# Column degrees from diagonals of products of the masked counts, in the middle stage of a graph kernel

## The chip, the cores and the metric

The kernel runs on one core of a Trainium2 chip. The metric is the device time of one execution in microseconds (us), the median of several runs. Engines are named as the profile names them: PE is TensorE (PEld its weight loads), DVE is VectorE, ACT is ScalarE, POOL is GpSimd, SP is SyncE, whose queue (SPq) issues the DMAs.

## What is computed

```python
# x (64, 128, 1024), adj (128, 128), bias (128), gumbel (1024*1024, 2)
h = relu(layernorm(x, axis=-1))                  # 64 batches of T=128 by N=1024
avg = h.mean(over the 64 batches)                # one vector of 128 per node, N=1024 nodes
x_norm = avg / norm(avg)
sim = (x_norm @ x_norm.T + 1) / 2
A = (sim + gumbel[:, 0] > 1 - sim + gumbel[:, 1])        # 1024 x 1024, zeros and ones
sym = clip(A + A.T, 0, 1); nmask = clip(sym + eye, 0, 1)
common = nmask @ nmask.T                         # counts of common neighbours
struct = where(sym and common > 1, common**2 / common.max(), 0)
W = A * struct
deg = W.sum(axis=0)                              # sum over the rows of each column
Wn = deg**-0.5 [row] * W * deg**-0.5 [column]
out = x + transpose(Wn applied to (h.T @ adj)) + bias
```

W is the square of (A times common), up to a constant. So a column's degree is the sum over rows of (A times common) squared: this is the quantity whose computation changes here.

## The kernel before

The work has three stages.

**Pass 1** (the span's start to about 108 us) reads all of x once, normalises, applies ReLU and sums the 64 batches into `S`; batches 0, 8, ... are also multiplied by the weight in fp32 (`kept`, 8 MATMULs of 128x128 per batch) and kept in `xw_res`.

**The middle stage** (about 108 to 193 us) makes the 1024x1024 matrix. It lies in 8 blocks of 128 rows.
- Comparisons: for each block `c`, PE makes `ps_sim` (fp32, 128x512), DVE first subtracts the two gumbel halves of a later block (`margin_of`) and then compares (`adjm`, L1007). PE's block `c` waits for DVE's comparison `c-2`, since `ps_sim` has two buffers.
- Symmetrised mask: PE adds a block and its transposed parts (`sym_start`, `sym_part`), ACT makes the even blocks of `nmask` (L441), DVE the odd ones (L1011), each with a row sum.
- `lonely_loops_dropped`: 8 small DVE operations on the diagonal blocks of `adjm` (L1035).
- Counts: PE multiplies `nmask` by itself, 16 MATMULs of 128x512 per block (L813), in the order `CHUNKS` = 0, 4, 1, 5, 2, 6, 3, 7. DVE multiplies each block with `adjm` into `masked` (`mask`, L1052).
- Degrees before the change: since DVE and ACT can only sum along a row, the columns' sums are had from turned blocks. As `common` is symmetric, column block `c` of (A times common), transposed, is `common` block `c` times A's transposed block. PE turns `adjm` (`turn_adj`, 8 MATMULs of 128x128, L778), ACT copies that to SBUF (`turned`, L545), DVE multiplies it with the counts a second time (`mask_t`, L1061), ACT squares and sums along the row (`degree_of`, L551).
- Then DVE bounds the degrees (L1066, L1067), POOL takes the power -1/4 (`roots`, L389: 6 columns, then 2), DVE finishes `qf` (L1072), PE spreads `qf` as rows over all partitions (`q_row`, L834), DVE multiplies (`rooted`, L1116), ACT squares and rounds (L594, L598), DVE takes the rest (`low`, L1122). PE gets zero products (`stay_awake`, L667) while it waits: `stay_awake(..., 5)` ahead of `q_row`, `(..., 8)` ahead of the first product. One fp32 MATMUL of the program is two records of the profile.
- Woven into this: the first pairs of batches of pass 2 are prepared. For a batch `j`, ACT makes ReLU twice (`relu2`, fp32 and fp16, L459, L469), DVE takes the fp16 rest (`h_low`, L1031), PE does 24 fp16 MATMULs (`xw_of`, L795), ACT copies the result to `z` (`z_of`, L489) and makes its fp16 part (`y_high_first`, L494; `y_high`, L508), DVE its rest (`y_low_first`, L1047; `y_low`, L1042).
- The maximum of the counts: `turn(0)`, `top_of(0)` on DVE, `spread(0)`, then `k0` on DVE (L1079, semaphore `top_count_read`).

**Pass 2** (from 193 us) multiplies 32 pairs of batches by the matrix, seven products per pair; almost all of it is PE's L852.

Each engine runs its own list in program order; the order is written by hand in each engine's function, with semaphores between them. SP's queue holds, behind the gumbel loads (L272), the loads of x for batches 1 to 7 (`x_first`, L286), which wait for all eight comparisons.

Of the kernel before, what the change touches and what calls it, by code (L numbers as in the profile page):

```python
# [28 lines left out]
BF16 = mybir.dt.bfloat16  # L29
# [23 lines left out]
def gnn_kernel(nc, x, adj, bias, gumbel, out):  # L53
# [14 lines left out]
    with ExitStack() as ctx:  # L68
# [16 lines left out]
        ident16 = sb("ident16", [P, P], BF16)  # L85
# [38 lines left out]
        adjm = xring[:, 0:4, :].bitcast(BF16).rearrange("p a (b n) -> p (a b) n", b=2)  # L124
        nmask = xring[:, 4:8, :].bitcast(BF16).rearrange("p a (b n) -> p (a b) n", b=2)
# [10 lines left out]
        def tile16(half, mat, k, dt=F16):  # L136
            return a16[:, half, mat, 2 * k:2 * k + 2, :].bitcast(dt).rearrange("p c n -> p (c n)")

        masked = [tile16(half, mat, k) for half, mat in ((0, 5), (1, 5), (1, 3), (1, 4)) for k in (0, 1)]
        adjt = [tile16(e // 4, 1 + e // 2 % 2, e % 2, BF16) for e in range(C)]  # L140
        masked_t = [tile16(0, 0, k) for k in (0, 1)]
        square_t = [a16[:, 0, m, :, :].bitcast(F32).rearrange("p c n -> p (c n)") for m in (3, 4)]
# [23 lines left out]
        ps_adjt = pair[2]  # L166
# [44 lines left out]
        s_adjtp = sem("adj_transposed")  # L211
        s_adjt = sem("adj_transposed_in_sbuf")
        s_m = sem("masked_count_ready")
        s_mt = sem("masked_count_transposed_ready")
# [37 lines left out]
        CHUNKS = [c + HC * k for c in range(HC) for k in (0, 1)]  # L252
# [7 lines left out]
        def _(sp):  # L260
# [49 lines left out]
        def _(pool):  # L310
# [85 lines left out]
            roots(0, 0, 6)  # L396
            roots(1, 6, C)
# [4 lines left out]
        def _(act):  # L402
# [20 lines left out]
            act.sem_inc(s_v, 3)  # L423
            def relus(i, except_for=()):
# [14 lines left out]
            for c in range(0, C, 2):  # L439
                act.wait_ge(s_sym, c + 1)  # L440
                nc.scalar.activation(nmask[:, c, :], ps_sym[c % 4], ACT.Sign,  # L441
                                     accum_out=row_count[:, c:c + 1]).then_inc(s_mask[0], 1)

# [99 lines left out]
            def turned(e):  # L543
                act.wait_ge(s_adjtp, e + 1)
                nc.scalar.activation(adjt[e], ps_adjt, ACT.Copy).then_inc(s_adjt, 1)  # L545

            def degree_of(e):
                act.wait_ge(s_mt, e + 1)
                if e >= 2:
                    act.wait_ge(s_deg, e - 1)  # L550
                nc.scalar.activation(square_t[e % 2], masked_t[e % 2], ACT.Square,  # L551
                                     accum_out=degree[:, e:e + 1]).then_inc(s_deg, 1)

            relu2(0, 0, 1)
            z_of(0, 0, 0)
            turned(0)
            y_high_first(0)
            turned(1)
            degree_of(0)
            relu2(0, 1, 0)  # L560
            z_of(0, 0, 1)
            y_high_first(1)
            turned(2)
            degree_of(1)
            relu2(0, 1, 1)
            turned(3)
            degree_of(2)
            y_high_first(2)
            y_high_first(3)
            turned(4)  # L570
            degree_of(3)
            z_of(0, 1, 0)
            y_high(0, 1, 0)
            turned(5)
            degree_of(4)
            z_of(0, 1, 1)
            y_high(0, 1, 1)
            turned(6)
            degree_of(5)
            y_high(0, 1, 2)  # L580
            turned(7)
            degree_of(6)
            relu2_wide(0, 2, 0)
            degree_of(7)
            relu2_high(0, 2, 0)
# [63 lines left out]
        def _(pe):  # L649
# [65 lines left out]
            for half in (0, 1):  # L715
                pe.wait_ge(s_rn, half + 1)
                bcast(ps_bc, rnorm, half).then_inc(s_bc, 1)
            for c in range(C):
# [7 lines left out]
                mm.then_inc(s_sim, 1)  # L726

# [14 lines left out]
            for k in range(C):  # L742
                pe.wait_ge(s_adj, k + 1)
                if k < 2:
# [26 lines left out]
            def turn_adj(e):  # L771

                if e == 0:
                    pe.wait_ge(s_edge, C)
                pe.wait_ge(s_adjt, e)
                c = CHUNKS[e]
                for k in range(C):
                    mm = nc.tensor.matmul(ps_adjt[:, k * P:(k + 1) * P], adjm[:, k, c * P:(c + 1) * P], ident16[:],  # L778
                                          start=True, stop=True, skip_group_check=True)
                mm.then_inc(s_adjtp, 1)  # L780

            def xw_of(i, q, b):
# [6 lines left out]
                if j > 1 or not isinstance(i, int) or i > 0:  # L789
                    pe.wait_ge(s_z, BODY * i + j)  # L790
                else:
# [10 lines left out]
            for e, c in enumerate(CHUNKS):  # L802
                if e >= 2:
                    pe.wait_ge(s_m, e - 1)
                    pe.wait_ge(s_mt, e - 1)
                for k in range(C):
                    if e == 0:
                        for n in {c % 2, k % 2}:
                            pe.wait_ge(s_mask[n], max(c, k) // 2 + 1)
                    if e >= 1 and k == HC:  # L810
                        turn_adj(e)
                    for m in range(2):
# [465 lines left out]
```

## Time and profile before

| | us |
|---|---|
| median of 3 runs | 853.83 (852.73 to 854.52) |
| profiled execution, its own time | 853.35 |
| its span, first to last instruction | 851.6 |
| busy in the span: PE, DVE, ACT, POOL | 821.1, 583.3, 508.4, 309.3 |
| mean granted TensorE clock | 0.994 of full speed |
| middle stage, comparisons' first MATMUL to first product of pass 2 | 115.08 to 193.12 |

The times in the rows count from the span's start. A timeline row gives start and duration, line, operation, operands and count; in brackets stands how long the engine had been idle and who released it. A duration holds the engine's pipeline tail, so that two instructions in a row overlap a little, and the step from start to start is what an instruction costs in a row of them. What lies outside the span (853.35 - 851.6 = 1.75 us) is taken as unchanged.

### The profile page before, as it was taken

The numbers are of one execution on the slowest core, as the hardware profiler recorded it, in microseconds if no ns is written. First come the engines' busy times: TensorE is split into PE (matmuls) and PEld (weight loads), VectorE is DVE, ScalarE is ACT, GpSimd is POOL, SyncE is SP. The second block draws the span as 40 slices with busy tenths as digits, with TensorE's granted clock in tenths as the row PEclk, the third lists the DMA queues.
The fourth block names the chain that finished last, engine by engine and source line by source line (L and its number), as shares of the span: only waits on it lengthen the run. The fifth ranks groups of instructions, "written<-read, shape, count | busy, mean of one in ns | idle before, by whom it ended". The sixth has DMA issues, their size and how long they took to land.

```text
span 851.6 us, 13546 instructions
## 1 busy us (share of the span) xinstructions
PE 821.1 (96%) x4739; PEld 429.6 (50%) x4746; DVE 583.3 (68%) x679; ACT 508.4 (60%) x530; POOL 309.3 (36%) x255
## 2 busy tenths in 40 slices
PE   4999999969999999999999999999999999999997
PEld 3545455554454555555455555554555455545553
DVE  7999986789986665666566666656665666566652
ACT  3888714879645665665566566656664555565531
POOL 4888710030433333333333333334333433333320
PEclk9999999989999999999999999999999999999999
DMA  8999913100553333333322223222222222233111
GB/s 346 408 409 345 421 46 124 50 1 1 214 183 126 106 109 107 124 106 108 103 99 99 99 99 99 99 99 99 99 99 99 99 99 99 99 101 111 60 50 74
DMA packets 30121, 113.14 MB, mean 133 GB/s; under 512 B 3472, under 2 KB 3600, under 8 KB 29072
## 3 DMA queue, kind: packets, MB, share of 16 engines
q1 hardware_dynamic: 30096, 112.80, 36.6%
q8 instruction: 16, 0.26, 0.1%
q14 instruction: 9, 0.07, 0.0%
HBM read 79.23 MB, written 33.55 MB: 132 GB/s over the span
## 4 chain that ended last, share of the span: by engine, by line
PE 80%; DVE 13%; issue 3%; ACT 2%; DMA 1%; DVEq 0%; SPq 0%; ACTq 0%
PE ps L852 65%; PE ps L795 8%; DVE stats L944 8%; PE ps L867 2%; PE ps L813 1%; PE ps L667 1%; DVE moments L950 1%; PE ps L724 1%; DMA out_dram<-obuf 1%; DVE ybuf L965 1%; DVE xring L1007 1%; DVE obuf L1198 1%; DVE ybuf L1042 0%; PE ps L738 0%; PE ps L731 0%
## 5 line engine op out<-in xcount | busy, mean ns | idle before, releaser
L852 PE MATMUL ps<-a,ybuf 128*128 128x512 f16 x2604 | 570.9, 379 | 0.5 <-ACT obuf L522 0.5
L852 PEld LDWEIGHTS ps<-a,ybuf 128*128 128x128 f16 x2604 | 252.6, 98 | 295.6 <-ACT obuf L522 1.0
L1042 DVE TENSOR_TENSOR ybuf<-zbuf,ybuf 128x1024 f16<-128x1024 f32 x124 | 164.5, 1327 | 157.4 <-ACT ybuf L508 157.4
L380 POOL TENSOR_TENSOR zbuf<-zbuf 128x512 f32<-128x512 f32 x31 | 40.9, 1318 | 444.1 <-ACT zbuf L489 444.1
L508 ACT ACTIVATE ybuf<-zbuf 128x1024 f16<-128x1024 f32 x124 | 117.8, 950 | 115.4 <-POOL zbuf L385 99.9
L522 ACT ACTIVATE obuf<-ps,bias_sb,w_out 128x512 f32<-128x512 f32 x62 | 47.9, 772 | 116.9 <-PE ps L852 111.7
L1031 DVE TENSOR_TENSOR hring<-hring 128x1024 f16<-128x1024 f32 x56 | 68.5, 1224 | 55.8 <-ACT hring L469 55.8
L795 PEld LDWEIGHTS ps<-w,hring 128*128 128x128 f16 x1344 | 79.5, 98 | 14.9 <-issue 2.4
L795 PE MATMUL ps<-w,hring 128*128 128x128 f16 x1344 | 84.2, 219 | 1.9 <-ACT zbuf L489 1.5
L1198 DVE TENSOR_TENSOR obuf<-obuf,xring 128x1024 f32<-128x1024 f32 x64 | 80.4, 1258 | 2.7
L383 POOL TENSOR_TENSOR zbuf<-zbuf 128x512 f32<-128x512 f32 x31 | 68.8, 2220 | 0.0
L489 ACT ACTIVATE zbuf<-ps 128x1024 f32<-128x1024 f32 x56 | 57.3, 1023 | 19.4 <-PE ps L795 19.2
L385 POOL TENSOR_TENSOR zbuf<-zbuf 128x512 f32<-128x512 f32 x31 | 67.8, 2186 | 0.0
L459 ACT ACTIVATE hring<-xring,nbias,rstd 128x1024 f32<-128x1024 f32 x49 | 60.1, 1227 | 0.0
L469 ACT ACTIVATE hring<-xring,nbias,rstd 128x1024 f16<-128x1024 f32 x49 | 60.1, 1227 | 0.0
L382 POOL TENSOR_TENSOR zbuf<-zbuf 128x512 f32<-128x512 f32 x31 | 50.8, 1638 | 2.4
L944 DVE BATCH_NORM_STATS2 stats<-xring 128x6 f32<-128x512 f32 x64 | 38.9, 671 | 0.7 <-issue 0.7
L696 PE MATMUL ps<-hring,ident 128*128 128x512 f32 x76 | 35.0, 607 | 0.3 <-ACT hring L412 0.3
L944 DVE BATCH_NORM_STATS2 stats<-ybuf 128x6 f32<-128x512 f32 x56 | 34.0, 666 | 0.0
L522 ACT ACTIVATE p<-ps,bias_sb,w_out 128x512 f32<-128x512 f32 x31 | 24.0, 773 | 10.4 <-PE ps L852 10.4
L1203 DVE SCALAR_TENSOR_TENSOR obuf<-ps,w_out,obuf 128x512 f32<-128x512 f32 x31 | 23.2, 750 | 9.8 <-PE ps L852 9.7
L696 PE MATMUL ps<-zbuf,ident 128*128 128x512 f32 x60 | 28.2, 602 | 1.7 <-ACT zbuf L412 1.5
(133 smaller groups left out, 673.1 us busy)
## 6 DMA issues: line engine op xcount, KB each, us to landing
xring<-in_x_dram SPq DMA_DIRECT2D x96, 512.0 KB, 4.6
out_dram<-obuf SPq DMA_DIRECT2D x64, 512.0 KB, 2.9
ybuf<-in_x_dram SPq DMA_DIRECT2D x28, 512.0 KB, 8.3
a<-in_L_gnn_gumbel_dram SPq DMA_DIRECT2D x7, 1024.0 KB, 15.9
obuf<-in_x_dram SPq DMA_DIRECT2D x11, 512.0 KB, 5.7
obuf<-in_L_gnn_gumbel_dram SPq DMA_DIRECT2D x1, 1024.0 KB, 23.9
w<-in_adj_dram SPq DMA_DIRECT2D x1, 64.0 KB, 1.9
bias_sb<-in_L_gnn_bias_dram SPq DMA_DIRECT2D x1, 0.5 KB, 2.1
```

The source lines that it names most:

```text
L383: nc.gpsimd.tensor_tensor(z[:, 6, :], z[:, 1, :], z[:, 0, :], ALU.subtract).then_inc(s_zs, 1)
L385: nc.gpsimd.tensor_tensor(z[:, 7, :], z[:, 2, :], z[:, 5, :], ALU.subtract).then_inc(s_zs, 1)
L459: nc.scalar.activation(h32, src, ACT.Relu, bias=nbias[:, bass.ds(t, 1)], scale=rstd[:, bass.ds(t, 1)]).then_inc(s_h32, 1)
L508: nc.scalar.activation(y16[:, q % 2, 0, a:a + n, :], z[:, a + 1:a + 1 + n, :], ACT.Copy).then_inc(s_yhi, 1)
L522: nc.scalar.activation(dst, src, ACT.Identity, bias=bias_sb[:, 0:1], scale=w_out[:, 0:1]).then_inc(s_v, 1)
L696: mm = nc.tensor.matmul(ps_avg[:, m], ident[:], h[:, m], start=False, stop=True, skip_group_check=True)
L795: mm = nc.tensor.matmul(ps_xw2[:, c * P:(c + 1) * P], h16[b][:, hk, c * P:(c + 1) * P], w16[:, wk, :], start=(hk == wk == 0), stop=(hk == ...
L852: mm = nc.tensor.matmul(bank[q % 2], y16[:, q % 2, yk, u, c * P:(c + 1) * P], a16[:, ak, mat, c, :], start=(start and c == yk == ak == 0), ...
L944: nc.vector.bn_stats(stats[:, j % 4, 6 * m:6 * m + 6], x1[j][:, m * H:(m + 1) * H]).then_inc(s_bn, 1)
L1031: nc.vector.tensor_tensor(h16[b][:, 1, :], h32, h16[b][:, 0, :], ALU.subtract).then_inc(s_hlo, 1)
L1042: nc.vector.tensor_tensor(y16[:, q % 2, 1, a:a + n, :], z[:, a + 1:a + 1 + n, :], y16[:, q % 2, 0, a:a + n, :], ALU.subtract).then_inc(s_y, 1)
L1198: nc.vector.tensor_tensor(ob, ob, xring[:, j, :], ALU.add).then_inc(s_out, 1)
```

## The change

1. **No turned adjacency.** `turn_adj`, `turned`, `mask_t` and ACT's `degree_of` go. Counts are made in the order 0 to 7 in full blocks. For each masked block, PE multiplies each of its 8 column blocks of 128x128 with itself (`squared`, 64 MATMULs in all) and sums over the blocks in PSUM: the diagonals of the 8 sums in `ps_diag` are the columns' degrees. DVE reads each diagonal with an identity and a sum along the row (new `degree_of`, 8 operations of 128x128).
2. The last masked block is made in two halves; the degrees' bounds and roots are split 4 and 4; `stay_awake` ahead of `q_row` goes from 5 to 10.
3. **Batch 1 in fp32.** Its load (`x_first[1]`) is issued when pass 1's sums are done and not after the comparisons. ACT makes its ReLU once (`first_h`), PE does 8 fp32 MATMULs with `w_unit` (`first_xw`), two behind each of the comparison blocks 2 to 5, and ACT and DVE make the first pair's `z` and `y` before and between the mask blocks. Batch 1's `relu2`, `h_low` and its 24 fp16 MATMULs go.
4. `adjm`, `nmask` and `ident16` are fp16 and no longer bf16 (both 16 bits).

```diff
@@ sync
+            sp.wait_ge(s_hpe, NT * (TRIPS1 + 1) - 2)
+            sp.dma_start(x_first[1], x[1]).then_inc(s_xf[1], 16)
             sp.wait_ge(s_adj, C)
-            for j in range(1, BODY):
+            for j in range(2, BODY):
@@ gpsimd
-            roots(0, 0, 6)
-            roots(1, 6, C)
+            roots(0, 0, HC)
+            roots(1, HC, C)
@@ scalar
-            relu2(0, 0, 1)
             z_of(0, 0, 0)
-            turned(0)
+            act.wait_ge(s_xf[1], 16)
+            nc.scalar.activation(first_h, x_first[1], ACT.Relu, bias=nbias[:, 1:2],
+                                 scale=rstd[:, 1:2]).then_inc(s_hhi, 1)
             y_high_first(0)
...
+            for c in range(0, C, 2):
+                act.wait_ge(s_sym, c + 1)
+                nc.scalar.activation(nmask[:, c, :], ps_sym[c % 4], ACT.Sign,
+                                     accum_out=row_count[:, c:c + 1]).then_inc(s_mask[0], 1)
@@ tensor
+            def first_xw(n):
+
+                pe.wait_ge(s_hhi, 1)
+                for c in (2 * n, 2 * n + 1):
+                    mm = nc.tensor.matmul(ps_xw2[:, c * P:(c + 1) * P], first_h[:, c * P:(c + 1) * P], w_unit[:],
+                                          start=True, stop=True, skip_group_check=True)
+                return mm
...
+                if 2 <= c < 6:
+                    mm = first_xw(c - 2)
+                    if c == 5:
+                        mm.then_inc(s_xw2, 1)
...
+            def squared(c, half):
+
+                pe.wait_ge(s_m, c + 1 + (half if c == C - 1 else 0))
+                for k in range(half * HC, (half + 1) * HC):
+                    mk = masked[c][:, k * P:(k + 1) * P]
+                    mm = nc.tensor.matmul(ps_diag[:, k * P:(k + 1) * P], mk, mk, start=(c == 0 and k % HC == 0),
+                                          stop=(c == C - 1), skip_group_check=True)
+                return mm
+
+            counted(0).then_inc(s_com, 1)
+            turn(0)
+            for c in range(1, C):
+                counted(c).then_inc(s_com, 1)
+                if c >= 2:
+                    for half in (0, 1):
+                        squared(c - 2, half)
+                if c == 1:
                     spread(0)
-                    xw_of(0, 0, 1)
-                if e == 3:
                     xw_of(0, 1, 0)
-                if e == 4:
+                if c == 3:
                     xw_of(0, 1, 1)
-            pe.wait_ge(s_m, C)
-            stay_awake(ps[:, 3, 0:P], 5)
+            for half in (0, 1):
+                squared(C - 2, half)
+            for half in (0, 1):
+                squared(C - 1, half).then_inc(s_diag, 1)
+            stay_awake(ps[:, 3, 0:P], 10)
@@ vector
             for c in range(1, C, 2):
+                y_low_first(c // 2)
                 dve.wait_ge(s_sym, c + 1)
...
+            def degree_of(c):
+
+                dve.wait_ge(s_diag, c // HC + 1)
+                m = slice(c * P, (c + 1) * P)
+                nc.vector.scalar_tensor_tensor(out=squares[:, m], in0=ps_diag[:, m], scalar=1.0, in1=ident[:],
+                                               op0=ALU.mult, op1=ALU.mult,
+                                               accum_out=degree[:, c:c + 1]).then_inc(s_deg, 1)
...
+            h_low(0, 1, 0)
             dve.wait_ge(s_edge, C)
             top_of(0)
             mask(0)
-            h_low(0, 0, 1)
...
-            mask_t(7)
-            mask(7)
-            root(0, 0, 6)
+            mask(7, LO)
+            mask(7, HI)
+            for c in range(HC):
+                degree_of(c)
+            bound(0, 0, HC)
+            for c in range(HC, C):
+                degree_of(c)
+            root(0, 0, HC)
+            bound(1, HC, C)
+            root(1, HC, C)
```

How the instructions stand on PE in the last three comparison blocks, before and then with the change (L724 before is L705 now, L731 and L733 are L716 and L718, L695 is `first_xw`):

```order
L724 MATMUL ps<-hring 128x512 [waits adj_ready]
L724 MATMUL ps<-hring 128x512
L724 MATMUL ps<-hring 128x512 [waits adj_ready]
L724 MATMUL ps<-hring 128x512
L724 MATMUL ps<-hring 128x512 [waits adj_ready]
L724 MATMUL ps<-hring 128x512
L731 MATMUL ps<-xring,ident 128x512 [waits adj_ready]
L731 MATMUL ps<-xring,ident 128x512
L733 MATMUL ps<-ident 128x128
L731 MATMUL ps<-xring,ident 128x512 [waits adj_ready]
```

```order
L705 MATMUL ps<-hring 128x512 [waits adj_ready]
L705 MATMUL ps<-hring 128x512
L695 MATMUL ps<-w_unit,hring 128x128 [waits h_high_ready]
L695 MATMUL ps<-w_unit,hring 128x128
L705 MATMUL ps<-hring 128x512 [waits adj_ready]
L705 MATMUL ps<-hring 128x512
L705 MATMUL ps<-hring 128x512 [waits adj_ready]
L705 MATMUL ps<-hring 128x512
L716 MATMUL ps<-xring,ident 128x512 [waits adj_ready]
L716 MATMUL ps<-xring,ident 128x512
L718 MATMUL ps<-ident 128x128
L716 MATMUL ps<-xring,ident 128x512 [waits z_ready,adj_ready]
```

Two fp32 MATMULs stand behind a block of comparisons, four times, and the second `sym_start` also waits for ACT's second `z_of`.

PE from the first block's maximum to the next counts, before and then with the change (L813, the counts, are L786 now; L796 is `squared`, L770 is `xw_of`):

```order
L764 MATMUL ps<-ident,col 1x128 [waits column_maxima_ready]
L778 MATMUL ps<-ident,xring 128x128 [waits adj_transposed_in_sbuf,lonely_loops_dropped]
L778 MATMUL ps<-ident,xring 128x128 x7
L813 MATMUL ps<-xring 128x512 x8
L778 MATMUL ps<-ident,xring 128x128 [waits adj_transposed_in_sbuf]
L778 MATMUL ps<-ident,xring 128x128 x7
L813 MATMUL ps<-xring 128x512 x8
L768 MATMUL ps<-top,ones 128x1 [waits top_ready]
L795 MATMUL ps<-w,hring 128x128 [waits top_count_read,h_low_ready]
```

```order
L751 MATMUL ps<-ident,col 1x128 [waits column_maxima_ready]
L786 MATMUL ps<-xring 128x512 x16
L755 MATMUL ps<-top,ones 128x1 [waits top_ready]
L770 MATMUL ps<-w,hring 128x128 [waits top_count_read,z_ready,h_low_ready]
L770 MATMUL ps<-w,hring 128x128 x23
L786 MATMUL ps<-xring 128x512 [waits masked_count_ready]
L786 MATMUL ps<-xring 128x512 x15
L796 MATMUL ps<-a 128x128 [waits masked_count_ready]
L796 MATMUL ps<-a 128x128 x3
```

A block's squares stand behind the counts of the block two later. DVE from the last masked block to `qf`, before and then with the change (`degree_of` is L1046, `mask` L1039):

```order
L1066 TENSOR_SCALAR degree_min<-degree 128x6 [waits degree_ready]
L1067 TENSOR_SCALAR has_deg<-degree 128x6
L1061 SCALAR_TENSOR_TENSOR a<-ps,a 128x1024 [waits degree_ready,adj_transposed_in_sbuf,common_ready]
L1052 SCALAR_TENSOR_TENSOR a<-ps,xring 128x1024 [waits common_ready]
L1072 TENSOR_TENSOR qf<-q_raw,has_deg 128x6 [waits q_raw_ready,degree_bounded]
```

```order
L1039 SCALAR_TENSOR_TENSOR a<-ps,xring 128x512 [waits common_ready] x2
L1046 SCALAR_TENSOR_TENSOR a,degree<-ps,ident 128x128 [waits column_squares_ready] x4
L1052 TENSOR_SCALAR degree_min<-degree 128x4 [waits degree_ready]
L1053 TENSOR_SCALAR has_deg<-degree 128x4
L1046 SCALAR_TENSOR_TENSOR a,degree<-ps,ident 128x128 [waits column_squares_ready] x4
L1058 TENSOR_TENSOR qf<-q_raw,has_deg 128x4 [waits q_raw_ready,degree_bounded]
```

Two full multiplications behind the last counts have become two halves of one and eight small ones.

## Rows read from the trace of the kernel before

**Rows 1.** Page, busy time of each engine in the span, its share and instructions
```profile
PE 821.1 (96%) x4739; PEld 429.6 (50%) x4746; DVE 583.3 (68%) x679; ACT 508.4 (60%) x530; POOL 309.3 (36%) x255
```

**Rows 2.** Chain of waits, end of the middle stage: start us, us, what
```profile
179.46 2.50 PE ps L667 x10
...
185.34 2.57 ACT xring L594 x4
...
221.77 1.34 PE ps L795 x24
```

**Rows 3.** Timeline of PE, pass 1's last fp32 products and the comparisons
```profile
106.07 1.95 PE L682 MATMUL ps<-w_unit,hring 128*128 128x128 f32 x16
...
122.97 1.98 PE L724 MATMUL ps<-hring 128*128 128x512 f32 x4 [0.28 <-DVE xring L1007]
...
127.50 3.70 PE L724 MATMUL ps<-hring 128*128 128x512 f32 x8 [0.28 <-DVE xring L1007]
```

**Rows 4.** Timeline of DVE, comparisons, masks and the dropped loops
```profile
133.11 1.23 DVE L1011 TENSOR_SCALAR_CACHE_REDUCE xring<-ps 128x1024 bf16<-128x1024 f32 x1 [0.64 <-PE ps L738]
134.26 0.08 DVE L1011 DVE_READ_ACCUMULATOR xring<-ps 128x1 f32 x1
134.98 1.23 DVE L1011 TENSOR_SCALAR_CACHE_REDUCE xring<-ps 128x1024 bf16<-128x1024 f32 x1 [0.63 <-PE ps L738]
...
140.26 2.19 DVE L1035 SCALAR_TENSOR_TENSOR xring<-ident,alone,xring 128x128 bf16<-128x128 bf16 x8
```

**Rows 5.** Timeline of PE, the counts
```profile
138.51 3.62 PE L813 MATMUL ps<-xring 128*128 128x512 bf16 x16
...
147.67 1.50 PE L795 MATMUL ps<-w,hring 128*128 128x128 f16 x24 [0.34 <-DVE k L1079]
...
163.75 1.50 PE L795 MATMUL ps<-w,hring 128*128 128x128 f16 x24 [1.53 <-ACT zbuf L489]
...
166.81 0.61 PE L778 MATMUL ps<-ident,xring 128*128 128x128 bf16 x8
167.26 3.62 PE L813 MATMUL ps<-xring 128*128 128x512 bf16 x16
170.71 0.61 PE L778 MATMUL ps<-ident,xring 128*128 128x128 bf16 x8
...
175.06 1.89 PE L813 MATMUL ps<-xring 128*128 128x512 bf16 x8
```

**Rows 6.** Timeline of DVE, from the last counts to the first rooted rows
```profile
149.85 0.68 DVE L1047 TENSOR_TENSOR ybuf<-zbuf,ybuf 128x512 f16<-128x512 f32 x1
...
180.64 0.16 DVE L1072 TENSOR_TENSOR qf<-q_raw,has_deg 128x2 f32<-128x2 f32 x1 [0.89 <-POOL q_raw L389]
...
180.91 1.23 DVE L1031 TENSOR_TENSOR hring<-hring 128x1024 f16<-128x1024 f32 x1
183.20 0.75 DVE L1116 SCALAR_TENSOR_TENSOR xring<-a,qf,ps 128x512 f32<-128x512 f16 x1 [1.06 <-PE ps L834]
```

**Rows 7.** Timeline of POOL, the roots
```profile
177.23 1.34 POOL L389 TENSOR_TENSOR q_raw<-degree_min,neg_quarter 128x6 f32<-128x6 f32 x1 [0.78 <-DVE has_deg L1067]
179.84 0.70 POOL L389 TENSOR_TENSOR q_raw<-degree_min,neg_quarter 128x2 f32<-128x2 f32 x1 [1.27 <-DVE has_deg L1067]
```

**Rows 8.** Stretches of 0.5 us: us, PE busy (instructions), PEclk, DMA share, GB/s
```profile
179.00:179.50 0.50, 0.04 (x1) 0.57 0.00 0
...
182.50:183.00 0.50, 0.50 (x7) 1.00 0.00 0
```

**Rows 9.** A stretch's busy us (instructions): PE, PEld, DVE, ACT, POOL; PEclk, DMA
```profile
214.00:240.00 26.00, 25.99 (x156) 13.05 (x154) 25.96 (x19) 14.17 (x15) 8.73 (x4) 1.00 0.67 246
```

**Rows 10.** Loads of x for batches 1 to 7 (L286), issue to landing
```profile
DMA to landing us min/median/max: 3.3/4.1/6.6
```

**Rows 11.** Loads of the gumbel values (L272), first and last start, issue to landing
```profile
L272 SPq DMA_DIRECT2D obuf<-in_L_gnn_gumbel_dram x1: 432/432/432, 87.6 to 87.6; - x1
...
DMA to landing us min/median/max: 9.9/16.9/23.9
```

More of the change, by code:

```diff
@@ L135, in gnn_kernel, with tile16 @@
         acc = zbuf[:, 0, :]
-        def tile16(half, mat, k, dt=F16):
-            return a16[:, half, mat, 2 * k:2 * k + 2, :].bitcast(dt).rearrange("p c n -> p (c n)")
+        def tile16(half, mat, k):
+            return a16[:, half, mat, 2 * k:2 * k + 2, :].rearrange("p c n -> p (c n)")
         masked = [tile16(half, mat, k) for half, mat in ((0, 5), (1, 5), (1, 3), (1, 4)) for k in (0, 1)]
-        adjt = [tile16(e // 4, 1 + e // 2 % 2, e % 2, BF16) for e in range(C)]
-        masked_t = [tile16(0, 0, k) for k in (0, 1)]
-        square_t = [a16[:, 0, m, :, :].bitcast(F32).rearrange("p c n -> p (c n)") for m in (3, 4)]
+        squares = a16[:, 0, 0, :, :].bitcast(F32).rearrange("p c n -> p (c n)")
+        first_h = hring[:, 0, :]
         rows_hi, rows_lo = xring[:, 4:8, :], xring[:, 0:4, :]
@@ L438, in _ @@
             keep(NK * TRIPS1 - 1)
[L439 to L442, printed above, removed]
             def relu2_wide(i, q, b):
@@ L743, in _ @@
                 pe.wait_ge(s_adj, k + 1)
+                if k == 1:
+                    pe.wait_ge(s_z, 2)
                 if k < 2:
@@ L788, in xw_of @@
                 pe.wait_ge(s_hlo, (BODY - 1) * i + j + 1)
-                if j > 1 or not isinstance(i, int) or i > 0:
-                    pe.wait_ge(s_z, BODY * i + j)
-                else:
+                pe.wait_ge(s_z, BODY * i + j)
+                if isinstance(i, int) and i == 0 and j == 2:
                     pe.wait_ge(s_cnt, 1)
@@ L801, in _, with counted @@
             pe.wait_ge(s_mask[1], 3)
[L802 to L805, printed above, removed]
+            def counted(c):
+                if c >= 2:
+                    pe.wait_ge(s_m, c - 1)
                 for k in range(C):
[L807 to L812, printed above, removed]
-                        mm = nc.tensor.matmul(ps_com[e % 2][:, m * H:(m + 1) * H], nmask[:, k, c * P:(c + 1) * P],
+                    if c == 0:
+                        for n in {0, k % 2}:
+                            pe.wait_ge(s_mask[n], k // 2 + 1)
+                    for m in (0, 1):
+                        mm = nc.tensor.matmul(ps_com[c % 2][:, m * H:(m + 1) * H], nmask[:, k, c * P:(c + 1) * P],
@@ L1007, in _, with y_low_first @@
                 nc.vector.tensor_tensor(adjm[:, c, :], ps_sim[c % 2], margin[c], ALU.is_gt).then_inc(s_adj, 1)
+            def y_low_first(u):
+                dve.wait_ge(s_yhi, u + 1)
+                nc.vector.tensor_tensor(y16[:, 0, 1, u, :], z[:, (u + 1) % 4, :], y16[:, 0, 0, u, :],
+                                        ALU.subtract).then_inc(s_y, 1)
             for c in range(1, C, 2):
+                y_low_first(c // 2)
                 dve.wait_ge(s_sym, c + 1)
@@ L1083, in _ @@
                                     ALU.mult).then_inc(s_cnt, 1)
+            h_low(0, 1, 1)
             mask(1)
-            y_low_first(0)
-            mask_t(1)
-            h_low(0, 1, 0)
+            y_low(0, 1, 0)
             mask(2)
-            mask_t(2)
-            y_low_first(1)
             mask(3)
-            mask_t(3)
-            h_low(0, 1, 1)
-            y_low_first(2)
-            y_low_first(3)
             mask(4)
-            mask_t(4)
+            y_low(0, 1, 1)
             mask(5)
-            mask_t(5)
-            y_low(0, 1, 0)
             mask(6)
-            mask_t(6)
-            y_low(0, 1, 1)
-            bound(0, 0, 6)
-            mask_t(7)
-            mask(7)
-            root(0, 0, 6)
-            bound(1, 6, C)
-            root(1, 6, C)
+            mask(7, LO)
[8 more added lines that the diff above has]
+            root(1, HC, C)
             dve.wait_ge(s_q, 2)
@@ L1113, in rooted @@
             def rooted(rows, k, half, c):
-                e, m = 2 * c + k, (LO, HI)[half]
+                e, m = HC * k + c, (LO, HI)[half]
                 nc.vector.scalar_tensor_tensor(out=rows[:, c, m], in0=masked[e][:, m], scalar=qf[:, e:e + 1],
```

91 lines of the change are left out of this document (19 added, 72 removed).

## Prediction

> **What bounds the kernel now.** The busy row comes first [rows 1]: PE is busy 96% of the span, so time is won only where PE works on less or waits less. The chain of waits then tells where the middle stage hangs: at its end the chain alternates between DVE, PE's zero products and ACT [rows 2], and behind it stands pass 2, PE's own. The stretch 214 to 240 has DVE busy for 25.96 and PE for 25.99 of 26 us [rows 9]: whatever arrives earlier at the first rooted rows is carried through pass 2's start by two full engines, and neither has slack that would eat it. So I price the change by one event, DVE's first `rooted` at 183.20 [rows 6], and by the first ACT square behind `kappa`, at 185.34 [rows 2]; both now end on what PE and DVE do after the last counts. The unit is the profiled execution, 853.35 us, 0.48 below the median; I take the same shift for both.
>
> **Comparisons.** Each block of four records lasts 1.98, a double block 3.70 [rows 3]: four records cost 1.72 and 0.26 is tail. With the idle 0.28 behind it a gap of 0.54 us is free per block while DVE sets the pace. Sixteen fp32 records of 128x128 last 1.95 [rows 3], so the four of one `first_xw` cost 0.43. They fit with 0.11 to spare: cost 0. If they did not fit at all, they would cost 4 x 0.43 = 1.7; below 0 they cannot go, as DVE's pace stays. I take 0, by the gap, which is of the same place. What is queued behind them are the comparisons themselves.
>
> Their input is batch 1's load, issued at about 106.1, when PE's last sum is done, behind the last gumbel load, which starts at 87.6 and lands 23.9 later, at 111.5 [rows 11]. A load of this size takes 3.3 to 6.6 from issue to landing [rows 10]. It lands at 111.5 to 118, and PE asks for it at 120.3 (a block of 1.72 and a gap before 122.97) [rows 3]. ACT stands idle there. Cost 0.
>
> **Masks.** DVE sits idle 0.64 before each odd mask block [rows 4]. `y_low_first` lasts 0.68 [rows 6], of which about 0.08 is tail (the accumulator read at 134.26 starts 1.15 behind an instruction of 1.23) [rows 4]: 0.60 in 0.64. Cost 0, at worst 0.2 for four. ACT's four `y_high_first` run when its `z` is made, before 131; PE's new wait for the second `z` is over by then. fp16 for bf16 is the same width: 0, unless zeros and ones in fp16 were slower on PE, for which 24 fp16 records in 1.50 beside 8 bf16 ones in 0.61, each with a tail, give no reason [rows 5].
>
> **Counts.** Before, from 138.51 to the end of the last counts (175.06 + 1.89, less 0.17 of tail, = 176.8) go 38.3 us [rows 5]. Work in it: 8 blocks of counts at 3.45 (167.26 to 170.71) = 27.6; 8 turns at 0.45 (166.81 to 167.26) = 3.6; 3 `xw_of` at 1.34 [rows 2] = 4.0; together 35.2. The other 3.1 are waits, the longest with 1.53 of idle at 163.75 for ACT, whose list was full of turned blocks and squares [rows 5]. With the change, up to the last counts: 27.6, squares of blocks 0 to 4 with 40 MATMULs of the turns' form, 5 x 0.45 = 2.25, 2 x 1.34 = 2.7, and one wait, PE to DVE to PE through `spread` and `k0`, 0.7 (the idle 0.34 at 147.67 and the tails on both sides) [rows 5]. Sum 33.2, so they end at 171.7: **5.1 earlier**. The wait at 163.75 goes because ACT has lost 8 copies and 8 squares; what is late next is nothing on PE: a block's squares come 3.5 us behind its mask. DVE now does `h_low` before `top_of(0)`, 1.15 more at 142.4, and has `top` at 143.8; PE needs it at 145.5.
>
> **From the last counts to `qf`.** Before: 176.8 to 180.64 [rows 6], 3.8. With the change, from 171.7: two half masks at the cost of a 512-wide operation with a PSUM operand (0.75, step 0.66) [rows 6], with 0.2 of signal: 173.2. PE's last squares end about 173.7, and DVE starts reading at 173.3. The price of a diagonal is not in the trace. Lower bound: the 128x128 operations on SBUF, 2.19/8 = 0.27 [rows 4]; upper: 0.66, a 512-wide one from PSUM. I take 0.27, the nearest form, with 0.08 of accumulator read [rows 4] and 0.02 for PSUM: 0.37. Four: 174.8; two bounds, 175.0; four more, 176.5; root and bounds, 176.8. POOL takes 0.70 for two columns and 1.34 for six [rows 7], so 1.0 for four: `qf` starts at 178.1. That is 6.4 instead of 3.8, **+2.6**, and `qf` stands 2.5 earlier.
>
> The Trainium skill ("VectorE: DVE Perf Modes", on the TRN2 errata) speaks against this part: every instruction pays a fixed latency, so many small tiles pay it each, and it gives 120 cycles plus the elements at 0.96 GHz for a PSUM source. By it, an estimate, a diagonal would be 0.26 and the eight, with reads, 2.7 us where I have 3.0; the sum would gain 0.3. No row of before has this operation.
>
> **From `qf` to rooted rows.** Before, `qf` was there at 180.8, but PE was still in its zero products: ten records from 179.46 lasted 2.50 [rows 2], since the granted clock had fallen to 1.2 GHz between 179.0 and 179.5, after PE had stood still from 177.0, and rose only after 182.5 [rows 8]. DVE, done with `h_low` (180.91 + 1.15) at 182.06, idled 1.06 until 183.20 [rows 6]. Now the twenty zero records start at 173.9 at full clock, 20 x 0.107 = 2.1, and are over at 176.0 (by 178.2 if much of them ran at half clock): they don't stand in front of `q_row`. At 2.4 GHz, eight records 0.86, tail and signals 0.4: rows in PSUM at 179.5. DVE is done with `h_low` at 179.6. So `rooted` starts at 179.6 and not 183.20: **3.6 earlier**. Behind it nothing has changed. Part of the executions will see some of a lowered clock, and I take 3.4.
>
> **Forecast:** 853.35 - 3.4 = 849.95 for the profiled execution, 850.4 against the median.
>
> **Rivals.**
> (a) *The clock falls again in PE's idle stretch before `q_row`.* For it: PE stands still from 176.0 to 178.1, and before it fell after 2.1 us of that [rows 8]. Against it: the zero products lengthen the busy part and end close to the need. Then `q_row` takes 1.7 at 1.2 GHz, its second half another 1.7, `spread(1)` follows at 182.0, and the first square behind `kappa` comes at about 183.0 instead of 185.34: 2.3 earlier, 851.5. The Trainium skill ("TensorE: Matmul & The Clock Gate", on why this matters for kernels) warns only of idle gaps between bursts longer than this one; by that rule this rival is out and 3.6 stands, 850.2. The trace disagrees, with 0.57 in the row after 2.5 us of idle. Chance 0.22.
> (b) *The gaps don't hold.* The margins are 0.11 and 0.04 us; if a wait's signal eats them, the four `first_xw` push the comparisons by up to 1.7: 852.1. Chance 0.08.
> (c) *The gain isn't carried,* or the edit doesn't shorten what it should: a later event that hangs on DMAs (reloads and stores around 220 to 240) keeps its time. Against: these are issued behind DVE's events, which move too. 853.8, chance 0.07.
> (d) *Slower: batch 1's load is late.* It is issued into the gumbel traffic; ACT waits for it in order, PE waits for ACT inside the comparisons, at 120.3. Every us of landing beyond 119 (ReLU 1.2) is a us of the whole. It decides from 122.4 on; landing at 125 costs 5.9 and makes 856.3. Against: that is 19 us after issue where 3.3 to 6.6 is seen [rows 10] and the gumbel loads end at 111.5. Chance 0.04.
> The forecast keeps 0.59.
>
> **Range.** Low: diagonals at 0.27 (8 x 0.10), POOL at 0.70: 1.1 and some 0.3 more than 3.4, 849.0. High: rival (a) with a POOL operation up to 0.9 longer, or (b): 852.4. Beyond 0.2% (1.7 us, about what a measurement of this kernel can tell) faster is below 852.1: forecast, (a), some of (b): 0.84. Same: rest of (b), (c): 0.11. Slower: 0.05.
>
> **What would show it.** In the profile after: idle before DVE's comparisons unchanged, the first counts at 138.5; squares' groups of 8 at 0.45; last counts ending near 171.7; no ACT copy between; diagonals at 0.37; `qf` near 178.1; `rooted` at 179.6, or 180.4 with PEclk at 0.5 there. It is wrong if the first counts start later than 139, if a diagonal costs over 0.5, or if PE gets idle stretches in pass 2 that it had not.

## The result, and the profile after

| | before | changed kernel |
|---|---|---|
| median, 6 runs each | 854.05 (852.70 to 855.64) | 849.62 (849.30 to 851.65) |
| ratio, 95% interval | | 0.9954 (0.9939 to 0.9970) |
| profiled execution, its span | 853.35, 851.6 | 849.50, 847.7 |

A second set of runs (below, `e0_after`) gave a ratio of 0.9953 (0.9939 to 0.9967). By the ratio the changed kernel is 0.46% or 3.9 us faster; the two medians of the table are 4.4 apart. One execution of `e7_both` below took 4944 us and is left out of its ratio. The two profiled executions differ by 3.85, and their traces can be laid on each other: pass 1 ends 0.1 earlier after the change.

The comparisons, timeline of PE after the change (start, duration, line, operands, count; in brackets the idle time ahead of it):

```profile
120.29 0.61 PE L695 MATMUL ps<-w_unit,hring 128*128 128x128 f32 x4
120.73 1.88 PE L705 MATMUL ps<-hring 128*128 128x512 f32 x4
122.45 0.61 PE L695 MATMUL ps<-w_unit,hring 128*128 128x128 f32 x4
122.90 1.96 PE L705 MATMUL ps<-hring 128*128 128x512 f32 x4
...
127.40 3.70 PE L705 MATMUL ps<-hring 128*128 128x512 f32 x8
```

Against [rows 3] the blocks start where they did: 122.97 became 122.90, and 127.50 became 127.40, the 0.1 of pass 1. The brackets with 0.28 of idle are gone: the fp32 products, 0.44 from start to start, stand in the gap. Only the first gap was too small. There PE had idled 0.15 before the change, and the block behind it, at 120.73, is 0.13 late; DVE's pace took that up within two blocks. The products' input was there long before. Timeline of ACT:

```profile
111.53 1.24 ACT L538 ACTIVATE hring<-obuf,nbias,rstd 128x1024 f32<-128x1024 f32 x1 [0.30 <-DMA obuf<-in_x_dram]
```

The load landed at 111.5 and ACT waited 0.30 for it, with PE asking at 120.3. The masks, timeline of DVE:

```profile
132.28 0.68 DVE L997 TENSOR_TENSOR ybuf<-zbuf,ybuf 128x512 f16<-128x512 f32 x1
133.01 1.23 DVE L1003 TENSOR_SCALAR_CACHE_REDUCE xring<-ps 128x1024 f16<-128x1024 f32 x1
134.16 0.08 DVE L1003 DVE_READ_ACCUMULATOR xring<-ps 128x1 f32 x1
134.16 0.69 DVE L997 TENSOR_TENSOR ybuf<-zbuf,ybuf 128x512 f16<-128x512 f32 x1
134.88 1.22 DVE L1003 TENSOR_SCALAR_CACHE_REDUCE xring<-ps 128x1024 f16<-128x1024 f32 x1
```

133.11 and 134.98 of [rows 4] are 133.01 and 134.88: each `y_low_first` fits ahead of its mask block. The counts, timeline of PE:

```profile
138.41 3.62 PE L786 MATMUL ps<-xring 128*128 128x512 f16 x16
141.87 0.27 PE L751 MATMUL ps<-ident,col 128*1 128x128 f32 x1
141.97 3.62 PE L786 MATMUL ps<-xring 128*128 128x512 f16 x16
145.52 0.38 PE L755 MATMUL ps<-top,ones 1*128 1x1 f32 x2
146.24 1.50 PE L770 MATMUL ps<-w,hring 128*128 128x128 f16 x24 [0.34 <-DVE k L1065]
147.58 3.62 PE L786 MATMUL ps<-xring 128*128 128x512 f16 x16
151.03 0.61 PE L796 MATMUL ps<-a 128*128 128x128 f16 x8
...
168.42 3.62 PE L786 MATMUL ps<-xring 128*128 128x512 f16 x16
171.87 1.35 PE L796 MATMUL ps<-a 128*128 128x128 f16 x20
173.42 0.40 PE L796 MATMUL ps<-a 128*128 128x128 f16 x4 [0.20 <-DVE a L1039]
173.66 2.45 PE L640 MATMUL ps<-ones,zeros 128*128 128x128 f32 x20
177.41 1.16 PE L821 MATMUL ps<-ident,qf 128*128 128x128 f32 x8 [1.30 <-DVE qf L1058]
```

Between 146.24 and 173.2 PE has no idle at all; the wait with 1.53 of idle at 163.75 [rows 5] is gone. The last counts end at 171.9, before at 176.8. Behind them, the timeline of DVE after the change:

```profile
172.07 1.29 DVE L1039 SCALAR_TENSOR_TENSOR a<-ps,xring 128x512 f16<-128x512 f32 x2 [2.67 <-PE ps L786]
173.28 0.28 DVE L1046 SCALAR_TENSOR_TENSOR a<-ps,ident 128x128 f32<-128x128 f32 x1
173.49 0.08 DVE L1046 DVE_READ_ACCUMULATOR a<-ps,ident 128x1 f32 x1
173.49 0.28 DVE L1046 SCALAR_TENSOR_TENSOR a<-ps,ident 128x128 f32<-128x128 f32 x1
...
177.19 0.16 DVE L1058 TENSOR_TENSOR qf<-q_raw,has_deg 128x4 f32<-128x4 f32 x1 [1.19 <-POOL q_raw L386]
...
178.61 0.74 DVE L1094 SCALAR_TENSOR_TENSOR xring<-a,qf,ps 128x512 f32<-128x512 f16 x1
```

and that of POOL, whose wait is the one for the bounds:

```profile
174.56 1.02 POOL L386 TENSOR_TENSOR q_raw<-degree_min,neg_quarter 128x4 f32<-128x4 f32 x1 [11.01 <-DVE has_deg L1053]
176.08 1.01 POOL L386 TENSOR_TENSOR q_raw<-degree_min,neg_quarter 128x4 f32<-128x4 f32 x1 [0.50 <-DVE has_deg L1053]
```

A diagonal costs a step of 0.21 (173.28 to 173.49): its accumulator read runs beside the next one. `qf` starts at 177.19, not 180.64 [rows 6]; `rooted` at 178.61 without idle, not 183.20 with 1.06. That is 4.59 earlier, and the first product of pass 2 is 4.60 earlier too (188.52, not 193.12). But the span gained 3.9. The rest is gone by the end of one wait, the one for the first stores of the output. Part of it PE had already lost in the 96 records of the first pair, before and after:

```profile
193.12 20.88 PE L867 MATMUL ps<-a,ybuf 128*128 128x512 f16 x96
188.52 21.19 PE L853 MATMUL ps<-a,ybuf 128*128 128x512 f16 x96
```

After the change PEclk is still at 0.50 up to 189 and the records take 0.31 longer; the products behind them start 4.30 earlier, not 4.60. The timeline of PE after the change, near 236:

```profile
236.64 2.76 PE L838 MATMUL ps<-a,ybuf 128*128 128x512 f16 x12 [0.94 <-ACT obuf L515]
```

and of ACT, which PE waits for there:

```profile
235.81 0.78 ACT L515 ACTIVATE obuf<-ps,bias_sb,w_out 128x512 f32<-128x512 f32 x1 [5.89 <-DMA out_dram<-obuf]
```

ACT may not overwrite an output buffer before its store has landed. The chain of waits shows that store, before and after (start, us, what):

```profile
234.68 4.90 DMA out_dram<-obuf
230.07 5.66 DMA out_dram<-obuf
```

It is issued behind DVE's work and goes out 4.61 earlier, but takes 0.76 longer to land. Before the change the same row of PE stood at 240.49 with 0.50 of idle; it is 3.85 earlier, not 4.60. As the store ended this wait, the 0.31 of the first pair cost nothing of its own. From there to the end both traces run alike.

### The profile page after: what moved, and what is told of

Same layout as the page of the kernel before. It is cut to its first block, busy times and chain, and to the rows that moved or that the text cites. A ratio compares the mean times of both kernels' runs of the same rounds, so it can differ in the third digit from the quotient of the medians.

```text
span 847.7 us, 13517 instructions
## 1 busy us (share of the span) xinstructions
PE 820.9 (97%) x4748; PEld 430.4 (51%) x4748; DVE 573.8 (68%) x687; ACT 491.6 (58%) x505; POOL 308.7 (36%) x255
## 4 chain that ended last, share of the span: by engine, by line
PE 86%; DVE 7%; issue 2%; ACT 1%; POOL 1%; DMA 1%; POOLq 0%; DVEq 0%; SPq 0%; ACTq 0%
PE ps L838 65%; PE ps L770 8%; DVE stats L930 4%; PE ps L786 3%; PE ps L853 2%; PE ps L669 2%; PE ps L705 2%; DMA out_dram<-obuf 1%; PE ps L640 1%; DVE obuf L1176 1%; DVE ybuf L951 1%; POOL rstd L333 0%; PE ps L723 0%; PE ps L655 0%; PE ps L716 0%
## 5 line engine op out<-in xcount | busy, mean ns | idle before, releaser
L770 PEld LDWEIGHTS ps<-w,hring 128*128 128x128 f16 x1320 | 78.1, 98 | 12.7 <-issue 0.4
L770 PE MATMUL ps<-w,hring 128*128 128x128 f16 x1320 | 82.7, 219 | 0.3 <-DVE k L1065 0.3
```

Of the source, the lines that this page charges most:

```text
L770: mm = nc.tensor.matmul(ps_xw2[:, c * P:(c + 1) * P], h16[b][:, hk, c * P:(c + 1) * P], w16[:, wk, :], start=(hk == wk == 0), stop=(hk == ...
```

## The experiments

Each ran beside the kernel before; the ratio is to that. "The changed kernel" is 0.9953 here.

**The two parts apart.** `e1_degrees_only` has the changed kernel's degrees and the old preparation of batch 1:

```diff
-                if 2 <= c < 6:
-                    mm = first_xw(c - 2)
...
-                    xw_of(0, 1, 0)
-                if c == 3:
-                    xw_of(0, 1, 1)
+                    xw_of(0, 0, 1)
+                if c == 3:
+                    xw_of(0, 1, 0)
+                if c == 4:
+                    xw_of(0, 1, 1)
```

> The changed kernel with batch 1 prepared as before (ReLU twice after the masks, 24 fp16 products among the counts, y_low_first among the masked blocks); degrees by diagonals stay. Theory P (the stage is PE's list plus its waits): the last counts end one xw_of (1.34) later than in the changed kernel, at about 173.1 instead of 171.9, and qf, the first rooted rows and the end move by the same: 2.5 to 2.6 faster than the kernel before, against 3.9 for both parts together. Rival B (batch 1 leaving the counts was the main thing, since it emptied ACT's and DVE's lists): this kernel gains less than 1.3.

Measured: 851.49, ratio 0.9973 (0.9963 to 0.9983), 2.3 faster than before. In its profile the first counts end 1.31 later than in the changed kernel's (143.18 and 141.87), because the clock was at 1.2 GHz for longer around the start of the comparisons: the spreading of rnorm took 3.62, not 2.88. The block of squares behind the last counts starts at 174.53, not 171.87: 1.35 later once the 1.31 is taken off, one `xw_of`. Theory P holds for this part. What the degrees' part is made of (the diagonals, the last block in halves, the roots split 4 and 4, the order of the counts, fp16) was not run apart; sixteen MATMULs of the counts last 3.62 in bf16 and in fp16.

`e2_batch1_only` is the kernel before with batch 1 moved:

```diff
+                if 2 <= c < 6:
+                    mm = first_xw(c - 2)
...
-                    xw_of(0, 0, 1)
```

> The kernel before with batch 1 alone prepared in fp32 in the comparisons; turned adjacency and second mask stay. Theory P, if the parts add up: 1.3 faster (one xw_of), since the rest of 3.9 belongs to the degrees. Rival A (ACT's full list was the cause of PE's waits in the counts: idle 1.53 at 163.75): ACT loses two ReLUs here and six small copies move ahead of the masks, some 6 us of its list, so PE's waits go too, and this alone gains 2.5 to 3.5, overlapping with the degrees' part.

Measured: 854.20, ratio 1.0002 (0.9991 to 1.0013): nothing. Both theories miss. The timeline of its PE shows where the time went:

```profile
146.91 0.38 PE L788 MATMUL ps<-top,ones 1*128 1x1 f32 x2
148.78 1.46 PE L832 MATMUL ps<-xring 128*128 128x512 bf16 x6 [1.50 <-DVE a L1080]
```

and that of its DVE why:

```profile
147.33 0.16 DVE L1097 TENSOR_SCALAR k<-ps 128x1 f32<-128x1 f32 x1 [3.48 <-PE ps L788]
147.41 1.22 DVE L1080 SCALAR_TENSOR_TENSOR a<-ps,a 128x1024 f16<-128x1024 f32 x1
```

Where the 1.34 of `xw_of` stood, PE now waits 1.50 for the first second mask (L1080). That is queued on DVE behind the wait for the counts' maximum, which PE sends only after the second counts. Batch 1's products had covered a wait. `e10_batch1_mask_first` moves one line:

```diff
             mask(0)
+            mask_t(0)
             dve.wait_ge(s_topb, 1)
             nc.vector.tensor_scalar(k0[:, 0:1], ...
-            mask_t(0)
```

> e2_batch1_only with DVE's first mask_t ahead of its wait for the maximum of the counts, nothing else. In e2 PE waits 1.50 for that mask_t (which stands behind the wait for the spread maximum), as long as the xw_of that had been there took (1.34). Theory Q (the batch's move gained nothing there because DVE's list, not PE's, led to the third counts): the wait of 1.50 goes and the kernel is 1.2 to 1.4 faster than the kernel before. Rival R (the ring of turned block, ACT's copy and second mask binds later in any case): PE's wait for ACT near 163 grows by what is won here, and the kernel stays the same as before.

Measured: 852.03, ratio 0.9979 (0.9968 to 0.9991), 1.8 faster than before. PE's wait of 1.50 is gone while the one for ACT stays as it was (1.43 in both). From the end of the first counts to the zero products behind the last mask it takes 35.66 (142.41 to 178.07), in e2 37.21 (141.92 to 179.13): 1.55 less. Theory Q holds; its 1.2 to 1.4 lies within the interval. The moved line was not run in the kernel before by itself; there the batch's products end at 149.0 and this mask at 148.7, so PE had no wait there for it to take away. So the two parts of the change add up only because the degrees' part removes this second mask: 2.3 alone, 0 alone, 3.9 together.

**The diagonals.** `e4_diag_extra` puts one more such operation, reading SBUF, ahead of each:

```diff
+                nc.vector.scalar_tensor_tensor(out=extra[:, m], in0=ones[:], scalar=1.0, in1=ident[:],
+                                               op0=ALU.mult, op1=ALU.mult,
+                                               accum_out=degree_x[:, c:c + 1])
```

> The changed kernel with 8 more operations of a diagonal's form and type (128x128 fp32, sum along the row), one ahead of each, that read SBUF in place of PSUM. It tells what a diagonal costs on the path and whether PSUM is the cheap or the dear source. Theory D: the diagonals stand on the path at the step of 0.21 seen in the changed kernel, so qf comes 8 x 0.21 = 1.7 later, with another 0.5 to 1.3 if the clock falls in PE's longer wait. My priced 0.37 would make 3.0. From SBUF the step would be 0.27 like the dropped loops' (2.19 for 8) if those are dear for their source; 0.21 or less if they are dear for their pointer scalar or because they work in place.

Measured: 851.46, ratio 0.9974 (0.9963 to 0.9986), 1.8 slower than the changed kernel. Its groups of DVE instructions in the stretch 172 to 178.5 (count, busy us, mean ns):

```profile
L1048 DVE SCALAR_TENSOR_TENSOR a<-ones,ident 128x128 f32<-128x128 f32 x8 | 2.3, 286 | 0.0
L1051 DVE SCALAR_TENSOR_TENSOR a<-ps,ident 128x128 f32<-128x128 f32 x8 | 2.3, 286 | 0.0
```

PSUM and SBUF sources last the same 286 ns, and the steps are 0.21 for both. The 0.27 of the dropped loops [rows 4] is not due to the memory; they differ in their pointer scalar, their type and in working in place, which was not taken apart. The last `qf` starts at 178.51 instead of 177.19, 1.32 later and not 1.7: in the changed kernel DVE idles 0.37 for the first root on POOL, and the extra operations fill that. The rest is the clock, which here fell in front of `q_row` (its eight records last 1.90, not 1.16). The interval overlaps the changed kernel's (0.9939 to 0.9967) by 0.0004; the 1.32 and the steps are read from the traces.

**The clock.** `e3_awake2`:

```diff
-            stay_awake(ps[:, 3, 0:P], 10)
+            stay_awake(ps[:, 3, 0:P], 2)
```

> The changed kernel with 2 in place of 10 zero products ahead of q_row. Theory C (clock): PE then stands still from about 174.2 to 177.4, 3.2 us; the granted clock falls to 1.2 GHz before or in q_row, the first rooted rows come 0.5 to 0.8 later and kappa 1.3 to 1.9 later: 1 to 1.9 slower than the changed kernel, 2 to 3 faster than the kernel before. Rival N (the zero products do nothing here): same as the changed kernel, 3.9 faster, PEclk 1.00 in q_row.

Measured: 850.52, ratio 0.9969 (0.9955 to 0.9984), by the ratios 1.4 slower than the changed kernel, though the intervals overlap. The profiled execution does what theory C says. Stretches of its PE (length in us, busy time and instructions of PE, PEclk, DMA share, GB/s):

```profile
175.00:176.00 1.00, 0.00 (x0) 1.00 0.00 0
176.00:177.00 1.00, 0.00 (x0) 0.78 0.00 0
177.00:178.00 1.00, 0.09 (x1) 0.50 0.00 0
```

and `q_row` in its timeline of PE:

```profile
177.91 2.08 PE L821 MATMUL ps<-ident,qf 128*128 128x128 f32 x8 [3.09 <-DVE qf L1058]
```

`q_row` takes 2.08 where it took 1.16. Counted from the start of the first counts (138.92 here, 138.41 in the changed kernel), `kappa` comes 1.84 later. So the mechanism is seen, and rival (a) is what happened in this execution without eight of the ten zero products; their worth in the median, 1.4, is not told from noise. The nine times lie in two groups, five from 849.19 to 850.52 and four from 851.79 to 852.10, with the profiled one in the upper. That would fit a clock that falls early in some executions only, but only one was profiled.

**What binds behind the first product.** `e5_ylow_early`, then `e6_awake4`, then both as `e7_both`; `e0_after` is the changed kernel beside them.

```diff
             mask(5)
+            y_low(0, 1, 2)
+            y_low(0, 1, 3)
             mask(6)
...
             h_low(0, 2, 1)
-            y_low(0, 1, 2)
-            y_low(0, 1, 3)
```
```diff
             pe.wait_ge(s_ahi, 1)
-            stay_awake(ps[:, 3, 0:P], 8)
+            stay_awake(ps[:, 3, 0:P], 4)
```

> The changed kernel itself, on the chip of the next three: 3.9 faster than before, with a store of out that lands 5 to 6 us after issue and an idle of PE of 0.5 to 1.0 us behind ACT's wait for it near 236.

> The changed kernel with y_low(0,1,2) and y_low(0,1,3) moved from the middle of the rounding (2.3 us of DVE's unbroken list) to between masks 5 and 6, where DVE idles 2.67. Theory S (from 182 to 236 DVE's list and the first stores of out end last; PE's idle of 0.94 is what is left of that): DVE comes 2.2 earlier to the stores, the idle of PE near 236 goes, and the kernel is 0.9 faster than the changed one; PE's start of the first product binds then, so not more. Rival T (that idle hangs on transfers that keep their time): same as the changed kernel.

> The changed kernel with 4 in place of 8 zero products ahead of the first product. They end at 188.7 while the first low part is there at 187.5: the first product starts about 0.9 to 1.1 earlier, at 187.7. Theory S: PE then only waits longer near 236 (idle 1.8 to 2.0), same time as the changed kernel. Rival E (PE's own start binds): 0.9 to 1.1 faster. If the clock is still at 1.2 GHz when the products begin, up to 1.7 of their first us run at half speed and the gain is gone from the start.

> Both edits together. Theory S: each frees the other, 1.8 to 2.0 faster than the changed kernel, 5.7 to 5.9 faster than the kernel before. Rival T or a low clock in the first products: no more than the better of the two alone, 0.9.

Measured: `e0_after` 849.43 (0.9953), e5 849.03 (0.9949, 0.9930 to 0.9968), e6 850.02 (0.9957), e7 850.14 (0.9959). None is told apart from the changed kernel. `e0_after` did as expected: its store landed in 5.5 and PE idled 0.82. e5's profile shows theory S in part: PE's idle near 236 fell from 0.94 to 0.18, but ACT still ended its wait on the store, which went out 0.23 earlier and not 2.2, and landed in 5.2. In e7 the gain of theory S is missing in the median; its fastest times, 847.28 and 847.36, reach it. e6's last condition came true, the low clock in the first products. In its timeline of PE the 96 records of the first pair took 23.70,

```profile
188.53 23.70 PE L853 MATMUL ps<-a,ybuf 128*128 128x512 f16 x96 [1.26 <-DVE a L1100]
```

and not 20.9. The same stretch of e6 by windows of 2 us, with the columns of e3's:

```profile
188.00:190.00 2.00, 1.47 (x4) 0.50 0.00 0
190.00:192.00 2.00, 2.00 (x6) 0.50 0.00 0
192.00:194.00 2.00, 2.00 (x6) 0.50 0.00 0
```

With PEclk at 0.50 the granted clock was at 1.2 GHz until 194. The four zero products themselves still ran at the full clock (eight records in 1.16, from 186.11); it fell behind them, between 187.0 and 187.5. In the changed kernel the low stretch, 185.5 to 189.5, lies mostly on its eight zero products; here all of it lies on idle time and on the first products. That suggested keeping it up, in `e8_fill_ylow`: e5 and

```diff
-            stay_awake(ps[:, 3, 0:P], 10)
+            stay_awake(ps[:, 3, 0:P], 14)
...
             xw_of(0, 2, 0)
+            stay_awake(ps[:, 3, 0:P], 17)
             pe.wait_ge(s_ahi, 1)
             stay_awake(ps[:, 3, 0:P], 8)
```

`e11_fill_only` is this without e5's edit. `e9_fill_all` is e8 with, at the end of pass 1,

```diff
             kept(TRIPS1 - 1, KEPT[-1])
+            stay_awake(ps[:, 5, 0:P], 4)
...
-            stay_awake(ps[:, 5, 0:P], 3)
+            stay_awake(ps[:, 5, 0:P], 5)
```

> The changed kernel with three edits: the two y_lows moved as in e5_ylow_early; 14 zero products for 10 ahead of q_row; and 17 zero products (3.7 us at full clock) put where PE stands still for 3.9 us ahead of the first product. Theory C (clock): the granted clock stays at 2.4 GHz from q_row to pass 2, the 8 zero products behind the wait last 1.73 and not 3.4, the first product starts at 187.6 when the first low part is there, and its 96 records last 20.7 in every execution; with the stores earlier as well this makes 848.0 or less in the median, 1.5 to 2.5 below the changed kernel, and a narrower spread. Rival Z (zero products don't count for the clock, or what is won waits for the stores near 236): same as e5, 849.0.

> As e8_fill_ylow, and at the end of pass 1 another 4 zero products ahead of the norms and 5 for 3 behind them. Theory C: the clock, which fell near 110.8 in every execution looked at, stays up, the spreading of rnorm lasts 1.8 and not 2.9, and the comparisons start 1.0 to 1.3 earlier: 847 or less. Rival: PE's products with one column at this place don't hold the clock up whatever stands around them, the longer list of zero products at half clock delays the spreading by up to 1.0: 849.

> e8_fill_ylow without the moved y_lows: the changed kernel with zero products only. Theory S (DVE's list and the first stores bind with PE's start no longer late): PE starts pass 2 0.9 earlier and idles 1.8 near 236, so the fastest executions gain nothing, but those in which the first products ran at half clock are gone: 0.2 to 0.8 below the changed kernel in the median. Rival E (PE's start binds): 0.9 to 1.5 below.

Measured: e8 847.96, ratio 0.9931 (0.9913 to 0.9949), runs from 847.26 to 849.42; e9 847.93, 0.9925 (0.9908 to 0.9943), 846.64 to 848.14; e11 849.50, 0.9952 (0.9934 to 0.9969). In e8 the clock stayed at 1.00 from q_row on, and pass 2 began as expected (timeline of its PE):

```profile
187.15 20.88 PE L854 MATMUL ps<-a,ybuf 128*128 128x512 f16 x96 [0.37 <-DVE a L1103]
...
235.41 2.76 PE L839 MATMUL ps<-a,ybuf 128*128 128x512 f16 x12 [1.40 <-ACT obuf L515]
```

Its PE reached 234.0 and then waited 1.40 for the store. Counted from the start of the first counts (137.84 in e8, 138.43 in e5), e8 started pass 2 0.80 earlier than e5, yet went on behind this wait at 97.57 where e5 did at 97.48: in these two executions all that the early start won went there. e9 and e11 started pass 2 as early by this count (49.31 behind the first counts, as in e8), and had no wait for a store there: theirs landed in 3.7 and 4.1, e8's in 5.5. So e11's idle of 1.8 near 236, which theory S had, did not occur. The zero products alone (e11) give nothing that can be measured, the moved `y_low`s alone next to nothing (0.4 of the medians); together the medians are 1.5 lower than `e0_after`'s, though the intervals of the ratios to before overlap (those of e9 and the changed kernel by 0.0004). e8 and e9 are the fastest versions run. In e9 the clock fell all the same between 112 and 114 (PEclk 0.50) and the spreading of rnorm took 3.54, not 2.88: its expectation at this place failed. In e8's profiled execution the clock did not fall there, with the list unchanged at that place, and its first counts began 0.57 earlier than the changed kernel's: a part of its time that its edits did not make. What decides there stays open.

## Why the prediction was right

The forecast was 850.4, within 849.0 to 852.4, a shift of 3.4; measured were 849.62 and a shift of 3.9 (by the ratio) or 3.85 (between the profiled executions). The steps up to `rooted` held but for one price; that the sum came so near was in part luck.

- **Comparisons and masks at 0:** right. Of the four blocks of comparisons behind fp32 products the last two start where they did, and so do the masks and the first counts, to 0.01 us once the 0.1 of pass 1 is taken off. The free gap of 0.54 held for three blocks; the first had 0.15 of idle and so 0.41, and its block came 0.13 late without effect. Rival (b) is out, and so is (d): batch 1's load landed at 111.5, where the working had it at the earliest.
- **Counts 5.1 shorter:** right. The sum had the last counts end at 171.7; they ended at 171.9, 4.9 earlier. The reason given for the lost wait near 163, ACT's list full of turned blocks and squares, holds: e1, without these, has no such wait, and e2 and e10, with them, still have 1.43. What it did not see is DVE's second mask behind the maximum's wait, which batch 1's products covered (e2, e10). The prediction counted batch 1's 1.34 as a gain of its own; by e2 it is one only together with the degrees' part. The sum didn't need to know that, the two parts apart would have.
- **Behind the last counts +2.6:** the step that was mis-sized. A diagonal was priced at 0.37, of which 0.08 for the accumulator read; it measured 0.21 and the read ran beside the next operation. Eight times 0.16 is 1.3, less DVE's idle of 0.37 for the first root, which the sum did not have: `qf` started at 177.19, 0.9 ahead of the 178.1 that was forecast. The lower bound had been 0.27, from a row that was dearer for a reason not seen. POOL's root was priced at 1.0 and took 1.02.
- **From `qf` to rooted rows:** 1.42 from `qf`'s start, forecast 1.5; the clock was at 2.4 GHz, so rival (a) did not occur in this execution. In e3 and e4 it did: in e3 `kappa` came 1.84 later, where the rival had put its first square 1.3 later.
- **Carried through:** the sentence that neither engine has slack that would eat the gain failed by 0.75. The stores' landing was not looked at: ACT waits for one, from its issue to its landing it took 5.7 against 4.9 before. Of the 0.75 PE lost 0.31 in the first pair, at the low clock, and 0.44 as idle there, which went from 0.50 to 0.94. A part of rival (c), then, beside the forecast. The DMAs were full in the 2 us in which the store was issued, but not only here: their share was 0.98 in the changed kernel, 1.00 before, and 0.99 in e9, whose store landed in 3.7. So why a store in one execution takes 3.7 and in another 5.7 is not settled.

The two errors, 1.0 too little at `rooted` and 0.75 too much behind it, went against each other, and the 0.2 that was taken off for a lower clock stood for neither. The time hit closer than its steps, and that was luck.

## What to carry to other kernels

Before pricing a part that is taken off the busiest engine, look at what its place in the list covers: in e2 PE lost 1.34 us of work and got 1.50 us of waiting, because another engine's list had its instruction behind a late wait. Work that fits the idle time between two waits (0.44 in 0.54, 0.60 in 0.64) cost nothing here, to hundredths of a microsecond; look at each gap, since the first one here was only 0.41. And follow a gain to the first transfer that someone waits for: what four engines carry on, a store can take back.

## What was not expected of the hardware

- A 128x128 fp32 operation with a sum along the row takes a step of 0.21 us on DVE from PSUM and from SBUF alike (286 ns each, sixteen of them in e4); its accumulator read adds nothing to the step. The Trainium skill ("VectorE: DVE Perf Modes", on the TRN2 errata) has a larger fixed part for PSUM sources; e4 doesn't show one in this form.
- In the kernel before the granted clock fell when PE had stood still for 2.1 us, in e3 when it had stood still for 1.7. In the changed kernel PE stood still from 181.4 to 185.3, and PEclk was at 1.00 all that time and fell only behind 185.5, when PE worked again; in e10 it did not fall in 2.5 us of idle at the place where it fell in the kernel before. Where it falls differs also between executions of the same list: the 96 records of the first pair took 21.2 us in the changed kernel and 21.4 in `e0_after`. With other zero products ahead of them they took 20.9 in e8 and 23.7 in e6.
- Work that is not needed can be worth time: with two zero products ahead of `q_row` in place of ten, `q_row` took 2.08 us and not 1.16 (e3).
- A store of 512 KB took 5.7 us from issue to landing where the median of the 64 stores in the same trace is 2.9 (changed kernel).
